# DLRM kernel: Z of four batches in one matmul, layer 0 of the preceding part between the halves

## Chip, cores and metric

The kernel runs on one core of a Trainium2 chip. The metric is the device time of one execution in microseconds. An engine here is TensorE (PE, its weight loads PEld), VectorE (DVE), ScalarE (ACT), GpSimd (POOL) or SyncE (SP).

## What is computed

A recommendation model for 2048 batches, all in float32. `_bn` normalizes over the batch.

```python
x = dense_inputs                                   # 2048 x 13
for W, b, g, be in bot:                            # 512, 256, 64
    x = _bn(jax.nn.relu(x @ W + b), g, be)
embs = tbl[idx]                                    # 26 tables of 12500 x 64, one row each per batch
T = jnp.concatenate([embs, x[:, None, :]], axis=1) # 27 x 64 per batch
Z = jnp.einsum('bnd,bmd->bnm', T, T)
R = jnp.concatenate([x, Z[:, iu, ju]], axis=1)     # upper triangle, 351 values
h = R
for W, b, g, be in top:                            # 512, 256, 1
    h = _bn(jax.nn.relu(h @ W + b), g, be)
return jax.nn.sigmoid(h)
```

## The kernel before

Each engine has its own instruction stream, written out by hand, in program order; semaphores tie them together. There is no planner.

**Start.** SyncE loads indices and weights (L288 to L300). VectorE turns indices into table rows and stages those of the first three parts (`stage_part`, L802), clears `Zs` (L814) and some constants. The bottom network runs over four chunks of 512 batches: layer 0 (L409), layer 1 with weights and activations split into two halves of the mantissa (`hi`, `lo`; L393, L399), layer 2 (L423). ScalarE does the relus (L610, L614, L582), VectorE the statistics (L827, L830, L720).

**Parts.** The 2048 batches are 16 parts of 128. GpSimd gathers the rows of a part with 26 indirect DMAs (L320; the last part L331) of 128 rows of 64 values each, in five loop passes of three parts (`LOOPS` = 5, `SLOTS` = 3 buffers `emb`) and the last part after it. A slot may be gathered into again once VectorE has run `stage_part` for it, which comes right behind the copies out of the transposes of the part that used it.

For each of the 15 parts in the loop:
- TensorE transposes 13 pairs of tables in four groups, each behind the landing of its gathers (L441), into two banks; VectorE copies each group to `TT` (L853); ScalarE adds the column of x (L636).
- TensorE multiplies: one matmul of 27 x 26 per batch (L455), 64 batches to a bank, the two halves h of the part from the lower and upper 64 rows of `TT`. The four column groups of the array take four batches side by side.
- Seven dummy matmuls keep TensorE working (`keep_clock`, L351), since its clock is granted by how it is used.
- VectorE and ScalarE take Z out of the banks into `Zs` (L254, L280), eight copies a half each.
- When all are taken, TensorE runs layer 0 of the top network on this part (L466 for x, L469 for the seven slices of `Zs`), four blocks of 128 outputs, each in a bank of its own. ScalarE writes two relus of each (L646, L648), VectorE statistics and the `lo` half (L864, L867).

**Last part.** It has a path of its own, in two halves of 64 batches (h = 0, 1) that are gathered one after the other: 13 gathers each, in groups of 8, 4 and 1 tables. Its transposes (h, g) are L479, its Z L493, its layer 0 L504 and L507 with batches as rows, transposed back by L516. The order on TensorE: transposes of half 0, Z 0, transposes (1,0), layer 0 of half 0, transposes (1,1) and (1,2), Z 1, layer 0 of half 1. Then comes the top network's layer 1 over all batches (L393, L399), layer 2 (L554), the normalization of the logits, the sigmoid (L699) and the store (L302).

**PSUM.** Eight banks: two for transposes, two for Z, four for layer 0, which also serve the dense layers as `out_bank`.

## Time and profile before

| | us |
|---|---|
| three timed runs | 589.98, 590.01, 588.6 (median 589.98) |
| profiled execution, span from first to last instruction | 987.2 |
| profiled execution, another time of its own | none on the page |
| TensorE busy in it | 448.2 (45%) |
| GpSimd busy | 401.1 (41%) |
| VectorE busy | 233.0 (24%) |
| ScalarE busy | 189.5 (19%) |

The profile is that of one execution, whose span is far longer than the timed runs. The timeline has for each run of like instructions its start, its length, the engine, the line, what it writes and reads, how many, and in brackets the idle time before it with what ended it.
### The profile page before, as it was taken

Reading aid. Unit: us, or ns where it says so; the run is one execution under the profiler, and the core shown is the slowest. Engines: PE = TensorE matmul, PEld = TensorE weight load, DVE = VectorE, ACT = ScalarE, POOL = GpSimd, SP = SyncE. Lnnn points to the kernel's source line nnn. Section 1 sums busy time; section 2 is a strip of 40 time slices with the busy share of each in tenths; the row PEclk is TensorE's granted clock in tenths of the full one; section 3 lists DMA queues with packets and bytes.
Section 4 is the critical chain, followed back from the end, with each engine's and each line's share of the span. In section 5 each row is a group of like instructions: output and inputs, shape, how many; then the busy total and the mean of one; then the engine's idle time right before and its main releaser. Section 6 shows DMA issues by size and latency. Waiting matters only on the chain.

```text
span 987.2 us, 13898 instructions
## 1 busy us (share of the span) xinstructions
PE 448.2 (45%) x5827; PEld 321.1 (33%) x5827; DVE 233.0 (24%) x640; ACT 189.5 (19%) x509; POOL 401.1 (41%) x426
## 2 busy tenths in 40 slices
PE   7751151624425161523517162351715244177787
PEld 3430020513214051412405051240514133165664
DVE  6600130402112040312204031220403022055542
ACT  5400020302011030302103030210303021044523
POOL 6777227072542707163361706336171634500000
PEclk9975575756657575755757575575757557577999
DMA  5122001020110202010110101011020101100000
GB/s 168 23 27 26 12 9 26 3 26 10 18 18 11 26 3 27 7 23 14 14 23 5 26 6 23 14 14 23 5 27 6 24 13 15 22 3 1 3 1 0
DMA packets 15895, 18.30 MB, mean 19 GB/s; under 512 B 7614, under 2 KB 8894, under 8 KB 15695
## 3 DMA queue, kind: packets, MB, share of 16 engines
q0 software_dynamic: 13312, 13.66, 10.6%
q1 hardware_dynamic: 2524, 3.72, 1.2%
q8 instruction: 53, 0.87, 0.4%
q14 instruction: 6, 0.05, 0.0%
HBM read 17.34 MB, written 0.01 MB: 18 GB/s over the span
## 4 chain that ended last, share of the span: by engine, by line
another core or an unknown queue 61%; PE 23%; ACT 10%; issue 3%; DVE 3%; DMA 0%; ACTq 0%; SPq 0%; DVEq 0%
PE l_bank L469 11%; ACT Zs L280 7%; PE l_bank L409 3%; PE l_bank L393 2%; PE l_bank L466 2%; PE l_bank L399 1%; PE l_bank L423 1%; ACT TT L636 1%; PE z_bank L455 1%; PE l_bank L507 1%; PE tr_bank L351 1%; DVE TT L853 1%; ACT hidden L582 0%; ACT hidden_hi L648 0%
## 5 line engine op out<-in xcount | busy, mean ns | idle before, releaser
L320 POOL DMA_INDIRECT emb<-table,stage x390 | 374.3, 960 | 424.1 <-DVE stage L802 309.2
L455 PE MATMUL z_bank<-TT 64*27 64x26 f32 x3840 | 127.5, 217 | 403.5 <-issue 388.4
L455 PEld LDWEIGHTS z_bank<-TT 64*27 64x27 f32 x3840 | 89.2, 132 | 442.9 <-issue 442.9
L254 DVE COPY Zs<-z_bank 27x112 f32<-27x112 f32 (+3 forms) x272 | 88.2, 324 | 498.7 <-remote 488.6
L280 ACT ACTIVATE Zs<-z_bank 27x112 f32<-27x112 f32 (+3 forms) x272 | 91.6, 337 | 552.8 <-remote 535.2
L469 PE MATMUL l_bank<-Zs,tw_sb 128*128 128x128 f32 x840 | 117.1, 298 | 0.0
L469 PEld LDWEIGHTS l_bank<-Zs,tw_sb 128*128 128x128 f32 x840 | 112.6, 215 | 0.0
L853 DVE COPY TT<-tr_bank 128x512 f32<-128x512 f32 (+1 forms) x60 | 51.1, 979 | 4.2 <-PE tr_bank L441 3.9
L351 PE MATMUL tr_bank<-idle_operand 128*128 128x512 bf16 x112 | 46.9, 590 | 0.0
L864 DVE BATCH_NORM_STATS2 stats_t<-h_block 128x128 f32 x60 | 17.7, 294 | 123.8 <-ACT hidden_hi L648 123.8
L441 PE MATMUL tr_bank<-ident,emb 128*128 128x128 f32 x195 | 30.8, 284 | 35.1 <-DVE TT L853 28.8
L646 ACT ACTIVATE h_block<-l_bank,par 128x128 f32<-128x128 f32 x60 | 22.0, 367 | 103.6 <-PE l_bank L469 103.6
L331 POOL DMA_INDIRECT emb<-table,stage x26 | 24.5, 944 | 34.0 <-DVE stage L802 26.3
L466 PE MATMUL l_bank<-x_all,twx_sb 128*128 x120 | 27.9, 318 | 21.7 <-ACT Zs L280 21.5
L340 POOL TENSOR_TENSOR hidden_lo<-h_block,hidden_hi 128x128 fp32r<-128x128 f32 x4 | 1.7, 454 | 88.2 <-ACT hidden_hi L681 88.2
L441 PEld LDWEIGHTS tr_bank<-ident,emb 128*128 128x128 f32 x195 | 21.9, 141 | 43.5 <-DVE TT L853 36.0
L393 PE MATMUL l_bank<-hidden_hi,w_hi 128*128 128x512 f32 x64 | 27.3, 426 | 17.4 <-issue 9.9
L466 PEld LDWEIGHTS l_bank<-x_all,twx_sb 128*128 128x128 f32 x120 | 21.0, 219 | 33.2 <-issue 33.2
L393 PE MATMUL l_bank<-hidden_lo,w_hi 128*128 128x512 f32 x64 | 26.6, 416 | 10.5 <-issue 10.5
L409 PE MATMUL l_bank<-hidden,bw_sb 13*128 13x512 f32 x32 | 27.7, 1061 | 5.4 <-DMA par<-params 5.4
L399 PE MATMUL l_bank<-hidden_hi,w_lo 128*128 128x512 f32 x64 | 19.8, 416 | 15.8 <-issue 15.8
L648 ACT ACTIVATE hidden_hi<-l_bank,par 128x128 f32 x60 | 21.6, 359 | 0.0
(120 smaller groups left out, 282.5 us busy)
## 6 DMA issues: line engine op xcount, KB each, us to landing
emb<-table,stage POOLq DMA_INDIRECT x416
tw_sb<-tw0x SPq DMA_DIRECT2D x1, 1792.0 KB
bw_sb<-bw SPq DMA_DIRECT2D x1, 512.0 KB
tw_sb<-tw SPq DMA_DIRECT2D x1, 512.0 KB
twx_sb<-twx SPq DMA_DIRECT2D x1, 256.0 KB
idx_raw<-idx SPq DMA_DIRECT2D x1, 169.0 KB, 3.0
bw_sb<-bw SPq DMA_DIRECT2D x2, 64.0 KB
hidden<-dense_t SPq DMA_DIRECT2D x1, 104.0 KB
```

The costliest lines, as they stand in the source:

```text
L254: last = copy(dst, src[:, :, ZC * q:ZC * q + w])
L280: return nc.scalar.activation(dst, src, ACT.Copy)
L320: pool.indirect_dma_start(out=emb[:, s, k, h, :], out_offset=None, in_=table, in_offset=bass.IndirectOffsetOnAxis(ap=stage[:, s, col:col + ...
L351: nc.tensor.matmul(bank[:, :], idle_operand[:, 0:P], idle_operand[:, :], start=True, stop=True)
L393: nc.tensor.matmul(bank, w1_scaled["hi"][:, k, o * P:(o + 1) * P], hidden0[part][:, k, ch * CHUNK:(ch + 1) * CHUNK], start=(n == 0 and par ...
L399: mm = nc.tensor.matmul(bank, w1_scaled["lo"][:, k, o * P:(o + 1) * P], hidden0["hi"][:, k, ch * CHUNK:(ch + 1) * CHUNK], start=False, sto ...
L409: nc.tensor.matmul(bank, bw0_sb[:, o * P:(o + 1) * P], dense_sb[:, ch * CHUNK:(ch + 1) * CHUNK], start=True, stop=True).then_inc(mm_done[" ...
L441: tr = nc.tensor.transpose(tr_bank[g % 2][:, c * P:(c + 1) * P], emb[:, s, k, :, :].rearrange("p h d -> p (h d)"), ident[:, :])
L455: mm = nc.tensor.matmul(bank[QUAD * j:QUAD * j + V, x * ZM:(x + 1) * ZM], one, one[:, 1:V], start=True, stop=True)
L466: nc.tensor.matmul(acc, twx_sb[:, cols], x_all[:, bass.ds(i * (2 * UNIT), 2 * UNIT)], start=True, stop=False)
L469: mm = nc.tensor.matmul(acc, tw0_sb[:, c, cols], Zs[:, c, :], start=False, stop=(c == ZC - 1))
L853: nc.vector.tensor_copy(TT[:, 0, :, n0:n0 + w].rearrange("p b n -> p n b"), tr_bank[g % 2][:, 0:w * UNIT].rearrange("p (n b) -> p n b", n= ...
```

## The change

The Z matmul takes four batches at once: stationary 128 columns (four batches of 32, `TT` padded from 27 to 32), moving 104 columns. The result is 128 x 104, and of it the four diagonal blocks of 27 x 26 are used. A part is cut in two sets of 64 batches, each of 16 such matmuls that alternate between the lower and upper 64 rows and are spread over four banks, so Z now has four banks. Layer 0 has two banks in the loop, taken in turn; blocks 2 and 3 wait for the relus of blocks 0 and 1. `Zs` gets three slots. TensorE's order becomes: transposes of part i, set 0 of i, layer 0 of part i-1, set 1 of i; the layer 0 of part 14 runs behind the loop. ScalarE and VectorE follow in the same order. The first three parts are written out ahead of a loop of four passes. The seven `keep_clock` matmuls of the loop are gone. The order of the batches within a part, of the dense inputs and of the output changes with it, so the sigmoid writes without a rearrangement. The last part's path keeps its operations.

```diff
-        TT = sb("TT", [P, 2, UNIT, V])
-        Zs = sb("Zs", [P, ZC, 2 * UNIT])
+        TT = sb("TT", [P, 2, UNIT, VP])
+        Zs = sb("Zs", [P, SLOTS, ZC, 2 * UNIT])
...
-        z_bank = [ps("z_bank%d" % k, [P, 512]) for k in range(2)]
-        l0_bank = [ps("l0_bank%d" % k, [P, 512]) for k in range(K0)]
+        z_set = ps("z_set", [P, ZB * 512])
+        z_bank = [z_set[:, k * 512:(k + 1) * 512] for k in range(ZB)]
+        l0_pair = [ps("l0_pair%d" % k, [P, 512]) for k in range(2)]
+        l0_bank = [l0_pair[0], l0_pair[1], z_bank[2], z_bank[3]]
...
+        def take_set(copy, s, t, quadrants):
+
+            for j in quadrants:
+                src = z_set[QUAD * j:QUAD * j + V, :].rearrange("p (k w) -> p k w", k=ZB)[
+                    :, :, 0:XB * NQ * ZM].rearrange("p k (u m) -> p k u m", m=NQ * ZM)
+                for q in range(NQ):
+                    w = quadrant_columns(q)
+                    dst = Zs[QUAD * q:QUAD * q + V, s, 0:w, t * UNIT:(t + 1) * UNIT].rearrange(
+                        "p c (k u j) -> p k u j c", k=ZB, j=NQ)[:, :, :, j, :]
+                    at = j * ZM + ZC * q
+                    last = copy(dst, src[:, :, :, at:at + w])
+            return last
...
+            def part_set(t):
+                for n in range(RX // SETS):
+                    k, g = divmod(n, XB)
+                    x = t * RX // SETS + n
+                    for h in range(2):
+                        four = TT[h * D:(h + 1) * D, 0, x * NQ:(x + 1) * NQ, :]
+                        mm = nc.tensor.matmul(z_bank[h * ZB // 2 + k][:, g * NQ * ZM:(g + 1) * NQ * ZM],
+                                              four.rearrange("p b n -> p (b n)"),
+                                              four[:, :, 1:V], start=True, stop=True)
+                mm.then_inc(z_done, 1)
+
+            def part_layer0(i, s):
+                for o in range(K0):
+                    cols = slice(o * P, (o + 1) * P)
+                    if o >= 2:
+                        pe.wait_ge(l0_relu, i * K0 + (o - 1))
+                    nc.tensor.matmul(l0_block_of(o), twx_sb[:, cols], x_all[:, bass.ds(i * (2 * UNIT), 2 * UNIT)],
+                                     start=True, stop=False)
+                    for c in range(ZC):
+                        mm = nc.tensor.matmul(l0_block_of(o), tw0_sb[:, c, cols], Zs[:, s, c, :],
+                                              start=False, stop=(c == ZC - 1))
+                    mm.then_inc(l0_done, 1)
+
+            def part(it, s, first=False):
+                i = it * SLOTS + s
+                part_transposes(it, i, s)
+                pe.wait_ge(tt_written, (i + 1) * GROUPS)
+                pe.wait_ge(tt_x_written, i + 1)
+                if not first:
+                    pe.wait_ge(z_taken_v, i * SETS)
+                    pe.wait_ge(z_taken_a, i * SETS)
+                pe.sem_inc(z_started, 1)
+                part_set(0)
+                if not first:
+                    if not (isinstance(i, int) and i == 1):
+                        pe.wait_ge(l0_relu, i * K0 - K0)
+                        pe.sem_inc(z_started, 1)
+                    part_layer0(i - 1, (s - 1) % SLOTS)
+                pe.wait_ge(z_taken_v, i * SETS + 1)
+                pe.wait_ge(z_taken_a, i * SETS + 1)
+                pe.sem_inc(z_started, 1)
+                part_set(1)
+
+            for s in range(SLOTS):
+                part(0, s, first=(s == 0))
+            with pe.Fori(1, LOOPS) as it:
                 for s in range(SLOTS):
...
-                    for h in range(2):
-                        bank = z_bank[h]
-                        for x in range(RX):
-                            for j in range(NQ):
-                                one = TT[h * D:(h + 1) * D, 0, x * NQ + j, :]
-                                mm = nc.tensor.matmul(bank[QUAD * j:QUAD * j + V, x * ZM:(x + 1) * ZM],
-                                                      one, one[:, 1:V], start=True, stop=True)
-                        mm.then_inc(z_done, 1)
-                    keep_clock(7, tr_bank[0])
...
+                    part(it, s)
+            pe.wait_ge(z_taken_v, LAST * SETS)
+            pe.wait_ge(z_taken_a, LAST * SETS)
+            pe.wait_ge(l0_relu, (LAST - 1) * K0)
+            part_layer0(LAST - 1, (LAST - 1) % SLOTS)
...
-            nc.scalar.activation(prob[:, :, :].rearrange("p b u -> p u b"),
-                                 logits[:, :].rearrange("p (u b) -> p u b", u=CU), ACT.Sigmoid,
+            nc.scalar.activation(prob[:, :], logits[:, :], ACT.Sigmoid,
...
-            nc.vector.memset(Zs[:, :, :], 0.0).then_inc(cleared, 1)
+            nc.vector.memset(Zs[:, :, :, :], 0.0).then_inc(cleared, 1)
+            nc.vector.memset(TT[:, :, :, V:VP], 0.0).then_inc(cleared, 1)
...
+            def part(i, s, first=False):
+                for g in range(GROUPS):
+                    n0, w = 2 * group_pairs(g)[0], 2 * len(group_pairs(g))
+                    dve.wait_ge(transposed, i * GROUPS + (g + 1))
+                    nc.vector.tensor_copy(
+                        TT[:, 0, :, n0:n0 + w].rearrange("p b n -> p n b"),
+                        tr_bank[g % 2][:, 0:w * UNIT].rearrange("p (n b) -> p n b", n=w),
+                    ).then_inc(tt_written, 1)
+
+                stage_part(s, bass.ds((i + SLOTS) * PW, PW))
+                dve.wait_ge(z_done, i * SETS + 1)
+                take_set(nc.vector.tensor_copy, s, 0, (0, 1)).then_inc(z_taken_v, 1)
+                if not first:
+                    part_stats(i - 1)
+                dve.wait_ge(z_done, i * SETS + 2)
+                take_set(nc.vector.tensor_copy, s, 1, (0, 1)).then_inc(z_taken_v, 1)
```

ScalarE's stream changes in the same way: x columns, takes of set 0, the relus of part i-1, takes of set 1, and the relus of part 14 behind the loop.

## Rows read from the trace of the kernel before

**Rows 1.** The page's first lines: span; busy us (share) and instructions.

```profile
span 987.2 us, 13898 instructions
...
PE 448.2 (45%) x5827; PEld 321.1 (33%) x5827; DVE 233.0 (24%) x640; ACT 189.5 (19%) x509; POOL 401.1 (41%) x426
```

**Rows 2.** The waits: engine, line, waited for: us in total, times, longest us.

```profile
PE z_bank L455 <- issue: 388.4, 368, 2.6
```

**Rows 3.** Timeline of PE, Z of part 1: start, us, engine, line, count, [idle before].

```profile
196.60 1.00 PE L455 MATMUL z_bank<-TT 64*27 64x26 f32 x67 [1.01 <-DVE TT L853]
...
220.58 0.20 PE L455 MATMUL z_bank<-TT 64*27 64x26 f32 x1 [2.60 <-issue]
```

**Rows 4.** Timeline of PE, part 14, no gather running; last line: a window, PEclk 0.50.

```profile
902.56 0.33 PE L441 MATMUL tr_bank<-ident,emb 128*128 128x128 f32 x1 [0.36 <-DVE TT L853]
903.90 1.71 PE L455 MATMUL z_bank<-TT 64*27 64x26 f32 x133 [1.01 <-DVE TT L853]
907.64 1.69 PE L455 MATMUL z_bank<-TT 64*27 64x26 f32 x123 [2.03 <-issue]
909.26 3.17 PE L351 MATMUL tr_bank<-idle_operand 128*128 128x512 bf16 x7
...
920.02 0.82 PE L479 MATMUL tr_bank<-ident,emb 128*128 128x128 f32 x6
...
904.00:912.00 8.00, 5.97 (x263) 3.89 (x262) 5.26 (x16) 5.37 (x16) 0.00 (x0) 0.50 0.02 4
```

**Rows 5.** Windows: us, busy of PE, PEld, DVE, ACT, POOL, PEclk, DMA share, GB/s.

```profile
57.00:108.00 51.00, 12.91 (x30) 6.75 (x28) 1.39 (x2) 1.37 (x2) 38.67 (x41) 0.56 0.20 26
...
950.00:973.00 23.00, 22.80 (x102) 18.55 (x103) 8.87 (x20) 5.36 (x10) 0.00 (x0) 1.00 0.00 1
```

**Rows 6.** Timeline of POOL: last of the first 78 gathers, first of the next.

```profile
107.00 0.94 POOL L320 DMA_INDIRECT emb<-table,stage  x1 [0.30 <-issue]
139.96 0.94 POOL L320 DMA_INDIRECT emb<-table,stage  x1 [32.01 <-DVE stage L802]
```

**Rows 7.** Timeline of PE: transposes (1,1), then (1,2), of the last part.

```profile
932.73 0.44 PE L479 MATMUL tr_bank<-ident,emb 128*128 128x128 f32 x2
933.00 0.27 PE L479 MATMUL z_bank<-ident,emb 128*64 128x128 f32 x1
```

**Rows 8.** Timeline, bottom layer 0: VectorE's L830 beside a gather.

```profile
17.98 0.67 DVE L830 TENSOR_TENSOR hidden_lo<-h_block,hidden_hi 128x512 fp32r<-128x512 f32 x1
18.07 1.39 POOL L320 DMA_INDIRECT emb<-table,stage  x1 [0.30 <-issue]
```

**Rows 9.** Timeline of PE, layer 0 blocks; windows: PE busy, PEclk the granted clock.

```profile
868.65 0.79 PE L466 MATMUL l_bank<-x_all,twx_sb 128*128 x2 [1.45 <-ACT Zs L280]
...
872.18 0.39 PE L466 MATMUL l_bank<-x_all,twx_sb 128*128 x2
...
873.96 0.39 PE L466 MATMUL l_bank<-x_all,twx_sb 128*128 x2
...
869.00:870.00 1.00, 1.00 (x6) 0.50 0.00 0
...
873.00:874.00 1.00, 1.00 (x12) 1.00 0.06 16
```

**Rows 10.** Timeline of ACT: eight takes of a half.

```profile
905.66 2.89 ACT L280 ACTIVATE Zs<-z_bank 27x112 f32<-27x112 f32 x8 [5.45 <-PE z_bank L455]
```

**Rows 11.** Timeline of DVE and POOL, start: clears, first statistics, a gather.

```profile
5.93 0.94 POOL L320 DMA_INDIRECT emb<-table,stage  x1 [0.31 <-issue]
6.01 0.81 DVE L814 MEMSET Zs<- 128x896 f32 x1 [0.25 <-DVE idx_clamped L797]
...
10.27 0.69 DVE L827 BATCH_NORM_STATS2 stats_b<-h_block 128x6 f32<-128x512 f32 x1 [2.81 <-ACT h_block L614]
```

**Rows 12.** Timeline of ACT, end: Square without, sigmoid with rearrangement.

```profile
980.80 0.72 ACT L694 ACTIVATE logit_sq<-logits,neg_mean 128x512 f32<-128x512 f32 x1 [0.73 <-DVE neg_mean L938]
...
983.68 1.30 ACT L699 ACTIVATE prob<-logits,norm_top 128x512 f32<-128x512 f32 x1
```

More of the change, by code:

```diff
@@ L68 @@
 ZM = NF
+VP = QUAD
+ZB = 4
+SETS = 2
+XB = 2 * RX // SETS // ZB
 CHUNK = 512
@@ new lines, in _, with part_relu @@
+            act.wait_ge(cleared, 2)
+            def part_relu(i):
+                for o in range(K0):
+                    act.wait_ge(l0_done, i * K0 + (o + 1))
+                    nc.scalar.activation(h0_part[:, o, :], l0_block_of(o), ACT.Relu,
+                                         bias=p_col("top", "b", 0)[:, o:o + 1]).then_inc(h0_f32, 1)
+                    nc.scalar.activation(hidden0["hi"][:, o, bass.ds(i * (2 * UNIT), 2 * UNIT)],
+                                         l0_block_of(o), ACT.Relu,
+                                         bias=p_col("top", "b", 0)[:, o:o + 1]).then_inc(l0_relu, 1)
@@ L653, in _ @@
+            for s in range(SLOTS):
+                part(s, s, first=(s == 0))
+            with act.Fori(1, LOOPS) as it:
+                for s in range(SLOTS):
+                    part(it * SLOTS + s, s)
+            part_relu(LAST - 1)
             for h in range(2):
@@ new lines, in part @@
+            def part(i, s, first=False):
+                for g in range(GROUPS):
+                    n0, w = 2 * group_pairs(g)[0], 2 * len(group_pairs(g))
[7 more added lines that the diff above has]
+                take_set(nc.vector.tensor_copy, s, 0, (0, 1)).then_inc(z_taken_v, 1)
+                if not first:
+                    part_stats(i - 1)
+                dve.wait_ge(z_done, i * SETS + 2)
+                take_set(nc.vector.tensor_copy, s, 1, (0, 1)).then_inc(z_taken_v, 1)
@@ L871, in last_stats @@
+            for s in range(SLOTS):
+                part(s, s, first=(s == 0))
+            with dve.Fori(1, LOOPS) as it:
+                for s in range(SLOTS):
+                    part(it * SLOTS + s, s)
+            part_stats(LAST - 1)
             def last_stats(o):
```

124 lines of the change are left out of this document (49 added, 75 removed).

## The prediction, before any run of the changed kernel

> **What bounds the kernel now.** I read the page first. Its span is 987.2 us, with TensorE busy 45% of it and GpSimd 41% [rows 1], and no other time stands on the page for this execution. The three timed runs have a median of 589.98 us, 397 us below that span, so the first question is what the profiled execution did that the timed ones can't have done.
>
> The waits answer it: TensorE stood idle before the Z matmuls of L455 for 388.4 us with nothing to wait for ("issue") [rows 2]. In the timeline the Z stage starts at full rate (67 records in 1.00 us), then crawls, at its worst with 2.60 us before a single record [rows 3]. The crawl lies where GpSimd issues gathers; the same stage of part 14, after the last gather, has one pause of 2.03 us [rows 4]. The bottom network's layer 1 crawls too: 30 matmul records in 51 us, while the same layer of the top network, with no gather about, does 102 in 23 us [rows 5]. A timed run 397 us shorter has no room for these stalls. I take them as something of the profiled execution alone.
>
> Without them, what is left? GpSimd. A gather takes 944 ns with 0.30 us before it, so one each 1.249 us. The 78 gathers of the first three parts end at 107.94 us. The next part waited in the trace for its slot until 139.96 us, 32.01 us long, because the bottom network was late [rows 6]. Unstalled, the crawling 30 records of the bottom network take 30/102 x 23 = 6.8 us instead of 51 [rows 5], so it ends at least 44 us earlier; the slot opens by 96 us, before 107.94, and GpSimd never waits. Then 338 more gathers run on to 108.2 + 338 x 1.249 = 530.4 us. From a part's last transpose to the next part's first one TensorE needs 17.4 us with no gather about (902.56 to 920.02 us [rows 4]), and a part's 26 gathers take 32.5 us: TensorE waits for landings, not the other way.
>
> After the last gather: its transpose stands at 933.00 us, the span ends at 987.2, so 54.2 us follow [rows 7]. 530.4 + 54.2 = 584.6 us. The 5.4 us up to the median hold the landing after the issue, what lies around the span, and gathers that meet a two-operand VectorE operation: in the bottom network they stretch to 1.40 us beside L830 [rows 8]. That this sum lands within 1% of the median is my best evidence that **the gather queue and the tail behind it bound the timed runs**.
>
> **The change, part by part.** All prices are from the profiled execution's rows; differences are added to the median, since the profiled span itself isn't comparable.
>
> *Z matmuls.* A part's 128 small matmuls (256 records, float32 makes two of each) become 32 of 104 columns (64 records). In the loop this is beside 32.5 us of gathers and worth nothing. The stage's own length: no row has this shape. A layer 0 record of 128 columns costs 3.53/16 = 0.22 us at the granted clock 0.50 (1.2 GHz) and 1.78/16 = 0.11 us at 1.00 (2.4 GHz) [rows 9], so a half (32 records of 104 columns) costs at most 5.7 or 2.9 us one after the other. But the old Z records overlap: 133 in 1.71 us at clock 0.50 is 13 ns each [rows 4], where streaming 26 columns at 1.2 GHz alone takes 22 ns. The new matmuls alternate between the two halves of the rows, so I take half: 2.8 us cold, 1.5 us warm, and keep the serial values for the range.
> The Trainium skill, page "TensorE: Matmul & The Clock Gate", section "Why this matters for your kernels", says that small-contraction matmuls in distinct row groups run concurrently. No row here shows row groups; by a rule of full concurrency the half is as I took it, and without it the sum would be 4.3 us higher.
>
> *keep_clock(7) removed:* 3.17 us of dummy matmuls a part [rows 4], which ran beside the copies. Worth nothing by itself; what it loses is that layer 0 starts at the low clock more often.
>
> *Layer 0 of the preceding part between the halves.* In the loop it stays under the gathers: per part about 25 us of TensorE chain (below) against 32.5. VectorE stages the slot's next rows as before, ahead of the takes, so GpSimd still never waits. *But at the end of the loop the order costs.* TensorE is in order, and the layer 0 of part 13 now stands behind the transposes of part 14, so behind its landing. Count t from the landing of part 14's last pair; the last part's final gather lands at 26 x 1.249 = 32.5, its group before at 31.2.
> Before: from that transpose (902.56) to the last part's first transposes (920.02) 17.4 us, on to its transposes (1,1) at 932.73 another 12.7 [rows 4, 7]. That is t = 30.1, before the landing at 31.2, so the gathers set the end: 32.5 + 54.2 = 86.7.
> After: 1.3 to the first half (902.56 to 903.90), 2.8 for it, then layer 0 of part 13: 3.5 for the first block cold and 3 x 1.8 [rows 9], making t = 13.0. ScalarE's eight takes (2.9 us [rows 10]) are done by 7.0, before the first block ends, so its relus don't hold the third block. Second half 1.5 warm, takes and handover 3.2: t = 17.7. Layer 0 of part 14, now wholly behind the takes: 2.8 for the first block, after 3 us of idling (between 1.8 warm and 3.5 cold, nearer the cold one) and 5.4: t = 25.9. The last part's first half then takes the unchanged 12.7: t = 38.6, past the last landing, and 54.5 more (932.73 to 987.2): 93.1. **The tail grows by 6.4 us.**
> Bounds: all at the high clock it is 4 us less; serial halves add 4.3; all of both layer 0s at the low clock would add 11 more, of which the range takes in the part up to 602.
>
> *Larger clears.* The memset of Zs takes 0.81 us and becomes three times that, the pads of TT (640 elements) some 0.6 us: 2.2 us more on VectorE, which is idle 2.81 us there before the first statistics [rows 11]. Hidden. If it held a gather up, 1 to 2 us would go straight to the end; beside the present memset the gather starting at 5.93 took 0.94 us as usual [rows 11], so I take 0. Waiting on `cleared` for 2 costs nothing by then.
>
> *Output order.* The sigmoid writes contiguously: 1.30 us now, against 0.72 us for a 128x512 Square without the rearrangement [rows 12]. It ends the chain: -0.6 us. Input layouts keep shapes and sizes: 0. The stride of TT going from 27 to 32 may move a copy's 0.98 us either way; in the loop it is hidden, in the tail few copies see it: 0, within 1 us.
>
> *Sum:* 589.98 + 6.4 - 0.6 = 595.8 us, about 1% slower.
>
> **Rivals.**
> *Slack hides it (no change).* If in the timed runs the part before last were landed earlier against the last gather than 32.5 us, or the half parts and layer 0 ran warm with shorter waits, the added layer 0 would fit. For this the new chain must shrink from 38.6 to under 32.5. For it: old chain (30.1) and landing (31.2) lie close together, and the new chain is a sum of six terms from other places. Against: a second layer 0 of over 7 us stands in a row, and the lowest bound still leaves 2.4 us. Or the old tail was already bound by TensorE, by some 5 us, which would explain the rest of 5.4 us between sum and median. Then 589.98 - 0.6 + 1 = 590.4. Chance 0.14.
> *TensorE bounds the loop in the timed runs too (faster).* If gathers are really quicker than the profile's 1.249 us and part of the "issue" stall is real, a part takes (590 - 96 - 67)/15 = 28.5 us now, with 96 as above and 67 the span from 920.02 to its end. The 32 matmuls cure the stall, a part falls to about 25 us (the chain above), and 15 x 3.5 = 53 us go: 537 us. This decides as soon as a gather takes under 28.5/26 = 1.10 us. Against it: all gathers outside the bottom network show 0.94 + 0.30 us to the hundredth. Chance 0.16.
> *The bigger matmuls save TensorE nothing:* three quarters of what they compute lies off the diagonal blocks and is unread. If they run one after the other at the low clock, a part's Z costs 11.5 us where the unstalled stage took about 5 [rows 4], and the time is some 600 us: the upper part of the forecast case, with its chance in it.
>
> **How the numbers follow.** The forecast case has 0.70, its own range 591.5 to 602. The range of 8 in 10 takes in the case without change: 588.5 to 602. The measurement can tell about 0.3% (1.8 us) from no change. Slower by more 0.70, within 0.14, faster 0.16.
>
> **What the profile of the changed kernel would show.** Right: gathers still spaced 1.249 us; TensorE's "issue" idle at Z far below 388 us, since a part leaves 141 matmul records instead of 340, and the span much nearer to the timed runs, which by itself says nothing of them. From the transpose of part 14's last pair to the last part's first transposes some 26 us where it was 17.4; the last part's transposes (1,1) without a wait for landing. Sigmoid near 0.7 us. Wrong: a timed result well under 588 us (gathers don't bound, or are quicker unprofiled); or the final gather landing after the first half of the last part was done, at a tail of 54 us behind it.

## The result, and the profile after

The changed kernel takes 595.73 us (median of four runs; its profiled execution 595.59), the kernel before 589.29 us (four runs). The ratio is 1.0100, 95% interval 1.0082 to 1.0118: slower by 1.0%, and by 6.4 us from median to median. One of the four runs was disturbed, at 811.9 us, and is not in the ratio; the median of the other three is 595.59. The unchanged kernel, profiled once more ("before, again"), has a span of 587.2 us where the first profile had 987.2, and its rows are used from here on. In every profile but that first one the time is 1.8 to 2.1 us above the span (595.59 for a span of 593.8, 589.28 for 587.2).

The page's first lines of the changed kernel, with the groups that answer to [rows 1, 2], and its chain of waits by engine. Columns as in [rows 1, 2]; in a group's row they are busy us, mean ns of one, and idle us ahead by what ended it.

```profile
span 593.8 us, 7908 instructions
...
PE 371.6 (63%) x2842; PEld 305.7 (51%) x2842; DVE 234.2 (39%) x641; ACT 190.8 (32%) x509; POOL 401.4 (68%) x426
...
POOL 62%; issue 21%; PE 10%; DVE 2%; ACT 2%; DMA 1%; POOLq 0%; DVEq 0%; ACTq 0%
...
L342 POOL DMA_INDIRECT emb<-table,stage x390 | 374.4, 960 | 121.8 <-issue 118.6
```

The waits of TensorE for landings in the changed kernel (us in total, times, longest):

```profile
PE tr_bank L461 <- DMA emb<-table,stage: 162.7, 33, 9.4
```

The same lines of the kernel before, profiled again:

```profile
span 587.2 us, 13898 instructions
...
PE 377.4 (64%) x5827; PEld 280.2 (48%) x5827; DVE 238.9 (41%) x640; ACT 190.5 (32%) x509; POOL 401.6 (68%) x426
...
PE tr_bank L441 <- DMA emb<-table,stage: 123.1, 27, 9.5
```

Two things are to be seen. TensorE's matmul records fell from 5827 to 2842, and its busy time by only 5.8 us, although 15 x 2.88 = 43 us of dummy matmuls are gone. The groups of the Z stage tell most of why, first before, again, then after (records, busy us, mean ns, idle ahead):

```profile
L455 PE MATMUL z_bank<-TT 64*27 64x26 f32 x3840 | 60.4, 220 | 32.9 <-issue 22.0 <-DVE TT L853 10.9
```

```profile
L472 PE MATMUL z<-TT 64*128 64x104 f32 x960 | 88.4, 355 | 14.0 <-DVE TT L917 11.0 <-ACT Zs L302 3.0
```

A quarter of the records, but 88.4 us of them in place of 60.4: the new Z stage is the longer one, even with the idle time counted in (102.4 against 93.3). The 28 us more of Z, and some 9 us more of layer 0 (L482 and L485 142.3 us, L466 and L469 133.1), take up most of the 43. TensorE now waits 162.7 us for landings instead of 123.1: what it was spared in the loop became waiting. The second is that the chain that ended last is gathers with the 0.30 us ahead of each (374.4 + 118.6 us, 83% of the span), then TensorE.

The two spans split at three places: the first one is the last transpose of part 14, the second one the last part's first transposes, the third one its transposes (1,1). Timeline of TensorE in the changed kernel, answering to [rows 4, 7] (start, us, engine, line, count, idle before):

```profile
499.35 0.47 PE L461 MATMUL tr_bank<-ident,emb 128*128 128x128 f32 x1 [1.37 <-DMA emb<-table,stage]
500.48 3.75 PE L472 MATMUL z<-TT 64*128 64x104 f32 x32 [0.65 <-DVE TT L917]
...
511.62 2.04 PE L472 MATMUL z<-TT 64*128 64x104 f32 x32
...
516.67 0.46 PE L482 MATMUL l_pair<-x_all,twx_sb 128*128 128x128 f32 x2 [3.02 <-DVE Zs L264]
...
525.52 0.82 PE L525 MATMUL tr_bank<-ident,emb 128*128 128x128 f32 x6
...
530.40 0.66 PE L525 MATMUL tr_bank<-ident,emb 128*128 128x128 f32 x4
...
540.10 0.44 PE L525 MATMUL tr_bank<-ident,emb 128*128 128x128 f32 x2
```

And the same of the kernel before, profiled again:

```profile
499.66 0.47 PE L441 MATMUL tr_bank<-ident,emb 128*128 128x128 f32 x1 [1.42 <-DMA emb<-table,stage]
500.72 2.08 PE L455 MATMUL z_bank<-TT 64*27 64x26 f32 x133 [0.59 <-DVE TT L853]
504.53 2.00 PE L455 MATMUL z_bank<-TT 64*27 64x26 f32 x123 [1.73 <-issue]
506.46 2.88 PE L351 MATMUL tr_bank<-idle_operand 128*128 128x512 bf16 x7
...
516.96 0.82 PE L479 MATMUL tr_bank<-ident,emb 128*128 128x128 f32 x6
526.12 1.11 PE L479 MATMUL tr_bank<-ident,emb 128*128 128x128 f32 x4 [3.90 <-DMA emb<-table,stage]
...
532.72 0.44 PE L479 MATMUL tr_bank<-ident,emb 128*128 128x128 f32 x2
```

| stretch, us | before, again | after | predicted for after |
|---|---|---|---|
| start to the last transpose of part 14 | 499.7 | 499.4 | no change |
| on to the last part's first transposes | 17.3 | 26.2 | 25.9 (17.4 before) |
| on to transposes (1,1) | 15.8 | 14.6 | 12.7 |
| on to the end of the span | 54.5 | 53.7 | 53.9 |

The last gather starts in both at the same time, first the kernel after, then before again (timeline of GpSimd):

```profile
529.24 0.95 POOL L353 DMA_INDIRECT emb<-table,stage  x1 [0.30 <-issue]
```

```profile
529.30 0.94 POOL L331 DMA_INDIRECT emb<-table,stage  x1 [0.31 <-issue]
```

So the loop neither gained nor lost. Before, TensorE waited 3.90 us for a landing at the transposes (1,0), at 526.12. They need the first eight gathers of the last half, the eighth of which is issued at 523.05:

```profile
523.05 0.94 POOL L331 DMA_INDIRECT emb<-table,stage  x1 [0.30 <-issue]
```

From 526.12 TensorE worked without a pause through layer 0 of half 0 to (1,1) at 532.72 and (1,2) at 533.00. So a landing set the tail, but not the last one: neither (1,1) nor (1,2) waited. After, (1,0) at 530.40 doesn't wait for a landing, and (1,1) stands 9.9 us behind the end of the last gather's issue (540.10 against 530.19), where it was 2.5 (532.72 against 530.24): the chain of TensorE and of the takes that it waits for sets the tail. The end has the sigmoid, answering to [rows 12], at 0.81 us against 1.30:

```profile
590.78 0.81 ACT L756 ACTIVATE prob<-logits,norm_top 128x512 f32<-128x512 f32 x1
```

### The profile page after: what moved, and what is told of

It is laid out like the page before. It is cut to its first block, busy times and chain, and to the rows that moved or that the text cites. A ratio compares the mean times of both kernels' runs of the same rounds, so it can differ in the third digit from the quotient of the medians.

```text
span 593.8 us, 7908 instructions
## 1 busy us (share of the span) xinstructions
PE 371.6 (63%) x2842; PEld 305.7 (51%) x2842; DVE 234.2 (39%) x641; ACT 190.8 (32%) x509; POOL 401.4 (68%) x426
## 4 chain that ended last, share of the span: by engine, by line
POOL 62%; issue 21%; PE 10%; DVE 2%; ACT 2%; DMA 1%; POOLq 0%; DVEq 0%; ACTq 0%
POOL emb L342 62%; PE l_pair L485 2%; PE l_pair L415 1%; PE z L415 1%; PE l_pair L553 1%; ACT Zs L302 1%; PE z L472 1%; PE z L421 1%; PE l_pair L421 1%; PE z L539 0%; DMA emb<-table,stage 0%; PE l_pair L482 0%; DVE Zs L264 0%; DVE moments_top L799 0%; DVE TT L291 0%
## 5 line engine op out<-in xcount | busy, mean ns | idle before, releaser
L342 POOL DMA_INDIRECT emb<-table,stage x390 | 374.4, 960 | 121.8 <-issue 118.6
L302 ACT ACTIVATE Zs<-z 27x112 f32<-27x112 f32 (+3 forms) x272 | 92.3, 339 | 259.6 <-PE z L472 253.2
L461 PE MATMUL tr_bank<-ident,emb 128*128 128x128 f32 x195 | 44.9, 363 | 175.2 <-DMA emb<-table,stage 162.7
L485 PE MATMUL l_pair<-Zs,tw_sb 128*128 128x128 f32 x840 | 113.4, 291 | 0.0
L264 DVE COPY Zs<-z 27x112 f32<-27x112 f32 x240 | 81.1, 338 | 76.2 <-PE z L472 73.4
L485 PEld LDWEIGHTS l_pair<-Zs,tw_sb 128*128 128x128 f32 x840 | 109.7, 210 | 0.0
L472 PE MATMUL z<-TT 64*128 64x104 f32 x960 | 88.4, 355 | 14.0 <-DVE TT L917 11.0
L472 PEld LDWEIGHTS z<-TT 64*128 64x128 f32 x960 | 82.4, 262 | 19.6 <-issue 17.9
L681 ACT ACTIVATE h_block<-l_pair,par 128x128 f32<-128x128 f32 x60 | 22.1, 368 | 55.1 <-PE l_pair L485 54.9
L482 PE MATMUL l_pair<-x_all,twx_sb 128*128 (+1 forms) x120 | 28.9, 328 | 3.0 <-DVE Zs L264 3.0
L482 PEld LDWEIGHTS l_pair<-x_all,twx_sb 128*128 128x128 f32 x120 | 21.1, 221 | 5.7 <-DVE Zs L264 3.2
L683 ACT ACTIVATE hidden_hi<-l_pair,par 128x128 f32 (+1 forms) x60 | 21.6, 360 | 0.0
L431 PE MATMUL l_pair<-hidden,bw_sb 13*128 13x512 f32 x16 | 14.6, 1066 | 5.6 <-DMA par<-params 5.6
```

The source lines that it names most:

```text
L264: last = copy(dst, src[:, :, :, at:at + w])
L302: return nc.scalar.activation(dst, src, ACT.Copy)
L342: pool.indirect_dma_start(out=emb[:, s, k, h, :], out_offset=None, in_=table, in_offset=bass.IndirectOffsetOnAxis(ap=stage[:, s, col:col + ...
L431: nc.tensor.matmul(bank, bw0_sb[:, o * P:(o + 1) * P], dense_sb[:, ch * CHUNK:(ch + 1) * CHUNK], start=True, stop=True).then_inc(mm_done[" ...
L461: tr = nc.tensor.transpose(tr_bank[g % 2][:, c * P:(c + 1) * P], emb[:, s, k, :, :].rearrange("p h d -> p (h d)"), ident[:, :])
L472: mm = nc.tensor.matmul(z_bank[h * ZB // 2 + k][:, g * NQ * ZM:(g + 1) * NQ * ZM], four.rearrange("p b n -> p (b n)"), four[:, :, 1:V], st ...
```

## The experiments

My theory: gathers carry the time up to the last landing; the change adds work of TensorE behind it, namely layer 0 of part 13. Rivals: the new Z matmuls are what costs (their length, or four banks that set 1 can't have before set 0 is taken); TensorE has a hand in the loop's time; the low clock in layer 0 of part 14 explains it.

### Is it the order or the new Z? (three kernels)

**Old order, new Z.** The changed kernel with layer 0 of part i-1 ahead of the transposes of part i. ScalarE's relus and VectorE's statistics move in the same way.

```diff
                 i = it * SLOTS + s
+                if not first:
+                    pe.wait_ge(z_taken_v, i * SETS)
+                    pe.wait_ge(z_taken_a, i * SETS)
...
+                    part_layer0(i - 1, (s - 1) % SLOTS)
                 part_transposes(it, i, s)
...
                 part_set(0)
-                if not first:
...
-                    part_layer0(i - 1, (s - 1) % SLOTS)
                 pe.wait_ge(z_taken_v, i * SETS + 1)
```

> The changed kernel, but layer 0 of part i-1 runs before the transposes of part i, on all three engines; the new Z matmuls, the two sets in the same four banks and all else stay. My theory (the tail grew through the order AND through two sets that wait for each other): counted from the transpose of part 14's last pair, 1.1 + set 0 3.7 + takes 3.1 + set 1 3.0 + takes 3.2 + layer 0 8.9 = about 23 us to the last part's first transposes, where the changed kernel has 26.2; so about 3 us less than the changed kernel, 592.5 us. Rival A (the order alone is to blame): all of it comes back, 588.7 us. Rival B (the bigger matmuls slow the whole loop): nothing comes back, 595.7 us.

Measured: 592.74 us against 588.84 of the kernel before on the same chip, ratio 1.0057 (1.0036 to 1.0078). Its timeline of TensorE:

```profile
499.31 0.47 PE L461 MATMUL tr_bank<-ident,emb 128*128 128x128 f32 x1 [1.36 <-DMA emb<-table,stage]
500.34 3.74 PE L472 MATMUL z<-TT 64*128 64x104 f32 x32 [0.56 <-DVE TT L918]
507.06 3.75 PE L472 MATMUL z<-TT 64*128 64x104 f32 x32 [2.98 <-ACT Zs L302]
...
523.41 0.82 PE L524 MATMUL tr_bank<-ident,emb 128*128 128x128 f32 x6
```

From the last transpose of part 14 to the last part's first ones it is 24.1 us, 6.8 above the 17.3 of before, although no second layer 0 stands there. Only 3.9 us of the 6.8 show in the time. The start is 0.3 us earlier, the next stretch is 1.5 us shorter, since its wait for a landing (3.90 us at 526.12 in before, again) is gone, and what follows is 1.1 shorter, half of it the sigmoid. Four banks for one set make set 1 wait for the takes of set 0, 2.98 us in the third line. The order before had one bank for each half and no such wait. The matmuls themselves add to it: the two sets take 7.5 us, the two halves of before 4.1.

**New order, old Z.** The changed kernel with the matmuls of 27 x 26, one bank for each half, still one half on each side of layer 0. The copies out of the banks are adapted to it.

```diff
             def part_set(t):
-                for n in range(RX // SETS):
-                    k, g = divmod(n, XB)
-                    x = t * RX // SETS + n
-                    for h in range(2):
-                        four = TT[h * D:(h + 1) * D, 0, x * NQ:(x + 1) * NQ, :]
-                        mm = nc.tensor.matmul(z_bank[h * ZB // 2 + k][:, g * NQ * ZM:(g + 1) * NQ * ZM],
-                                              four.rearrange("p b n -> p (b n)"),
-                                              four[:, :, 1:V], start=True, stop=True)
+                for x in range(RX):
+                    for j in range(NQ):
+                        one = TT[t * D:(t + 1) * D, 0, x * NQ + j, :]
+                        mm = nc.tensor.matmul(z_bank[t][QUAD * j:QUAD * j + V, x * ZM:(x + 1) * ZM],
+                                              one[:, 0:V], one[:, 1:V], start=True, stop=True)
```

> The changed kernel's order, banks, slots and layouts, but Z by the old matmuls of 27 x 26, one bank a half, taken half by half. My theory: the deferred layer 0 stays in the tail, so the chain is 1.1 + 2.5 + 9 + 2 + 3.2 + 8.9 = 26.7 us and the time that of the changed kernel, 595.7 us within 1. Rival (the bigger matmuls cost the time): back to about 589 us.

Measured: 594.26 us, ratio 1.0098 (1.0078 to 1.0117). That is a little below the window I had put down. Its timeline of TensorE:

```profile
498.81 0.47 PE L459 MATMUL tr_bank<-ident,emb 128*128 128x128 f32 x1 [1.42 <-DMA emb<-table,stage]
...
524.93 0.82 PE L520 MATMUL tr_bank<-ident,emb 128*128 128x128 f32 x6
```

26.1 us: with the new order the chain has its whole length with either form of Z.

**Both old**, in the frame of the changed kernel: `Zs` with three slots, `TT` with stride 32, the larger clears, three parts written out ahead of the loop, the new batch order and sigmoid, no dummy matmuls in the loop. The edit is the two above together, without the wait between the halves.

> Both taken back in the changed kernel's frame: layer 0 of part i-1 before the transposes of part i, old Z matmuls, the second half not waiting for the takes of the first. What stays of the change: padding, three slots of Zs, two banks for layer 0 in the loop, no keep_clock in the loop, batch order and a contiguous sigmoid. My theory: the tail chain is again about as long as the landing of the last gather leaves (30 to 32 us), so 589.3 - 0.5 for the sigmoid = 588.8 us, up to 1 us more for a colder layer 0. Rival (padding, slots, bank sharing or the missing dummy matmuls cost the time): above 592 us.

Measured: 588.43 us, ratio 1.0000 (0.9986 to 1.0014). Last transpose of part 14 to the next first ones: 17.8 us.

```profile
499.46 0.47 PE L459 MATMUL tr_bank<-ident,emb 128*128 128x128 f32 x1 [1.42 <-DMA emb<-table,stage]
...
517.25 0.82 PE L516 MATMUL tr_bank<-ident,emb 128*128 128x128 f32 x6
```

Everything else in the change is worth nothing together (within the interval of 0.14%; the sigmoid's 0.5 us is in it), so what is left is these two parts. The ratio is to the kernel before, run beside it; that of the changed kernel comes from another comparison (589.29 us for before) than those of the three others (588.84):

| | old Z | new Z |
|---|---|---|
| old order | 588.43 us, ratio 1.0000, chain 17.8 | 592.74 us, ratio 1.0057, chain 24.1 |
| new order | 594.26 us, ratio 1.0098, chain 26.1 | 595.73 us, ratio 1.0100, chain 26.2 |

Each alone costs 4 to 6 us, and together not the sum: in the new order, the ratios show no cost of the new Z. There, layer 0 of part 13 fills the time in which set 1 would wait for its banks. In the tail that is all that the reorder buys, and it is bought with a layer 0 there: 7.5 us for a wait of 3.

### Is it the clock in layer 0 of part 14?

Six dummy matmuls ahead of that layer 0, in the 3 us in which TensorE waits for the takes.

```diff
                     part(it, s)
+            keep_clock(6, tr_bank[0])
             pe.wait_ge(z_taken_v, LAST * SETS)
```

> The changed kernel with six dummy matmuls behind the loop, ahead of the wait for the last takes, where TensorE idles 3.0 us. My theory: layer 0 of part 14 takes 7.1 us instead of 8.9 and all of it shows in the end, since that layer 0 stands on the chain: 594.0 us, 1.7 less than the changed kernel. Rival (the last landing sets the end, the layer 0 is hidden): 595.7 us.

Measured: 593.90 us, ratio 1.0086 (1.0063 to 1.0110). From its timeline of TensorE:

```profile
514.79 1.47 PE L373 MATMUL tr_bank<-idle_operand 128*128 128x512 bf16 x6
517.87 0.46 PE L482 MATMUL l_pair<-x_all,twx_sb 128*128 128x128 f32 x2 [1.61 <-DVE Zs L264]
...
525.09 0.82 PE L526 MATMUL tr_bank<-ident,emb 128*128 128x128 f32 x6
```

That layer 0 now takes 7.2 us (517.87 to 525.09) instead of 8.85, as expected. How much of it reaches the time is less sure: the median is 1.8 us below that of the changed kernel, but the ratios, 1.0086 and 1.0100, have intervals that overlap. At most 1.8 us of the 6.4 are the clock here; the rest is not.

### Do the two row halves of TensorE work side by side?

The changed kernel with the 16 matmuls of a set in another order: eight of the lower 64 rows, then eight of the upper. Same work, same banks.

```diff
-                for n in range(RX // SETS):
-                    k, g = divmod(n, XB)
-                    x = t * RX // SETS + n
-                    for h in range(2):
+                for h in range(2):
+                    for n in range(RX // SETS):
+                        k, g = divmod(n, XB)
+                        x = t * RX // SETS + n
```

> The changed kernel with the 16 matmuls of a set ordered by half: eight on the lower 64 rows, then eight on the upper, instead of alternating. If neighbouring matmuls overlap because they sit in different rows of the array, a cold set grows from 3.7 to about 5.7 us and a warm one from 2.0 to 2.9, and the tail by 2 to 4 us: 597.5 to 599.5 us. If the overlap doesn't come from that, set and time stay: 595.7 us.

Measured: 603.48 us against 589.99, ratio 1.0237 (1.0212 to 1.0263), which is 7.7 us over the changed kernel and more than I expected. From its timeline of TensorE:

```profile
500.52 0.47 PE L461 MATMUL tr_bank<-ident,emb 128*128 128x128 f32 x1 [1.42 <-DMA emb<-table,stage]
501.64 6.40 PE L472 MATMUL z<-TT 64*128 64x104 f32 x32 [0.65 <-DVE TT L917]
...
516.88 3.46 PE L472 MATMUL z<-TT 64*128 64x104 f32 x32
...
532.96 0.82 PE L525 MATMUL tr_bank<-ident,emb 128*128 128x128 f32 x6
```

A set costs 6.40 us cold and 3.46 warm; alternating, 3.75 and 2.04. Taking turns makes the same matmuls 1.7 times as fast, at either clock (PEclk 0.50 for the cold sets, 1.00 for the warm ones). That the rows alone do it isn't shown: each row half writes its own two banks, so matmuls that take turns between row halves take turns between PSUM banks as well. My serial bound (5.7 and 2.9 us, from layer 0 records of 128 columns) was itself 12 to 20% low. Of the 6.2 us by which the chain is longer (32.4 against 26.2), the two sets are 4.1; layer 0 between them took 8.9 us (507.97 to 516.88) instead of 7.5, that behind them 9.6 instead of 8.85, and the last gather came 1 us late.

### Does TensorE have a hand in the loop?

The kernel before with 21 dummy matmuls where it has 7.

```diff
-                    keep_clock(7, tr_bank[0])
+                    keep_clock(21, tr_bank[0])
```

> The kernel before with 21 instead of 7 dummy matmuls a part, 14 x 0.22 to 0.44 us = 3 to 6 us more on TensorE behind Z in each part, of which some 1 lies under the takes. My theory: hidden under the gathers 14 times, seen once, in part 14, less the slack of 1 to 2 us before the last landing: 590 to 594 us. Rival (TensorE bounds the loop): 15 x 3 to 6 us more, 630 to 680 us.

Measured: 592.44 us against 589.99, ratio 1.0039 (1.0017 to 1.0061), in five runs between 588.28 and 593.67. The profiled one is that of 588.28. Timelines of TensorE, then GpSimd:

```profile
504.97 6.29 PE L351 MATMUL tr_bank<-idle_operand 128*128 128x512 bf16 x21
```

```profile
528.87 0.95 POOL L331 DMA_INDIRECT emb<-table,stage  x1 [0.30 <-issue]
```

3.4 us more for each of 15 parts (6.29 against 2.88) is 51 us of dummy matmuls. TensorE's busy time grew by 39.9 us (417.3 against 377.4), since transposes and layer 0 took less (L441 36.9 for 41.9 us, L469 103.6 for 106.0), and its waits for landings at L441 fell from 123.1 to 89.8 us. The last gather is where it was: in the loop TensorE has time to spare. Where the median lost 2.4 us can't be read from a profile whose own run lost nothing, and stays open.

### Is a gather's issue the price of the loop?

The other side: the kernel before with one more gather for each of the 15 loop parts, into a buffer of its own, ahead of the part's last transpose.

```diff
                             ).then_inc(landed[s][k // GROUP], 16)
+                    pool.indirect_dma_start(
+                        out=extra_rows[:, s, :], out_offset=None, in_=table,
+                        in_offset=bass.IndirectOffsetOnAxis(ap=stage[:, s, 25:26], axis=0),
+                    ).then_inc(landed[s][GROUPS - 1], 16)
```

> The kernel before with one more gather in each of the 15 parts of the loop, into an unused tile; the last group's transpose waits for it too. My theory (gathers bound the timed runs of the kernel before): 15 x 1.249 = 18.7 us more, 608 us. Rival (TensorE bounds its loop): about 589 to 591 us.

Measured: 607.60 us against 588.77, ratio 1.0317 (1.0293 to 1.0341): 18.8 us, where 15 x 1.249 = 18.7. The last gather starts 18.9 us later:

```profile
548.16 0.95 POOL L336 DMA_INDIRECT emb<-table,stage  x1 [0.30 <-issue]
```

**The kernel before, again**, unchanged, for a profile that is worth reading:

> The kernel before, unchanged, profiled once more. My theory (the idle time marked issue in the profile shown belongs to that one execution, not to the kernel): the span is now near 587 us, the issue stall at the Z matmuls is gone, GpSimd issues without a wait, and the tail from the transpose of part 14's last pair to the last part's first transposes is about 17 us. Rival (records of 256 Z matmuls a part always stall a profile): a span near 987 us again.

Measured: 588.42 us, ratio 0.9997 (0.9984 to 1.0009). Its rows stand above. A part leaves 340 records, as before, and the crawl of [rows 2, 3] is gone: 22.0 us of "issue" at L455, where it was 388.4. Why the first profiled execution crawled isn't known.

### Why are some gathers 1.40 us long?

In the bottom network gathers last 1.40 us beside L830 [rows 8]. There the gather queue itself could be shortened. L830 subtracts two operands that both lie in SBUF. The kernel before, with ScalarE's relu of layer 0 written to a PSUM bank that is free then, so that one operand comes from there:

```diff
-                nc.scalar.activation(h0_block[:, n % 2, :], bank, ACT.Relu,
+                nc.scalar.activation(z_bank[n % 2][:, 0:CHUNK], bank, ACT.Relu,
...
-                nc.vector.bn_stats(stats["bot", 0][:, o, ch, :], h0_block[:, n % 2, :])
+                nc.vector.bn_stats(stats["bot", 0][:, o, ch, :], z_bank[n % 2][:, 0:CHUNK])
...
-                nc.vector.tensor_tensor(hidden0["lo"][:, o, cols], h0_block[:, n % 2, :],
+                nc.vector.tensor_tensor(hidden0["lo"][:, o, cols], z_bank[n % 2][:, 0:CHUNK],
```

> The kernel before, but in the bottom network's layer 0 ScalarE writes the float32 relu into the two idle Z banks instead of the block in SBUF, so the subtraction on VectorE that makes lo has only one operand in SBUF. My theory (a gather can't start while a VectorE operation with two SBUF operands runs, and gathers bound the kernel): the gathers of 1.40 us become 0.94, 17 x 0.46 = 7 to 8 us less, if the tail follows: 581.5 to 583 us. Rival A (the stretch has another cause, the weight loads for one): gathers still at 1.40, 589 us. Rival B (gathers don't bound): gathers at 0.94 and 589 us all the same.

Measured: 584.20 us against 589.99, ratio 0.9904 (0.9884 to 0.9925). The lines that answer to [rows 8], in its timelines of GpSimd and VectorE, and its last gather:

```profile
18.32 0.94 POOL L320 DMA_INDIRECT emb<-table,stage  x1 [0.30 <-issue]
523.28 0.94 POOL L331 DMA_INDIRECT emb<-table,stage  x1 [0.30 <-issue]
...
17.91 0.67 DVE L830 TENSOR_TENSOR hidden_lo<-z_bank,hidden_hi 128x512 fp32r<-128x512 f32 x1
```

The subtraction itself is as long as before, 0.67 us. The gather beside it falls from 1.40 us (1.39 in [rows 8]) to 0.94, the last gather starts 6.0 us sooner (523.28 against 529.30), and the time follows by 5.8. Over the whole loop the gathers are busy 368.8 us (mean 946 ns) instead of 374.8. I had expected 7 to 8 us, from 17 stretched gathers; in before, again, 13 last 1.34 us or more, which gives the 6.0.

The edit also moves ScalarE's write and the read of the statistics out of SBUF, so by itself it doesn't say which of the three mattered. The gathers of before, again, do. Of 15 that start while L830 runs, 13 are stretched. Of 11 that start while L867 runs, which subtracts two SBUF operands too but is only 0.27 us long, four are, to 1.00 to 1.04 us. The 12 that start beside the statistics of L864, with one operand in SBUF, and the 30 that start beside ScalarE's relus L646 and L648, take 0.94 to 0.95.

### Put together

**Old Z, old order, relu in PSUM**, in the frame of the changed kernel:

> old_z_old_order and before_relu_in_psum together. My theory: both effects stand side by side, the gathers end 5.8 us earlier and the sigmoid saves 0.5: 582.9 us, ratio to before 0.989 or less. Rival (the tail's TensorE chain, no longer than the landing by a hair, takes over): 584 to 585 us.

Measured: 582.72 us, ratio 0.9888 (0.9869 to 0.9907).

**The same with the clock kept up:** the seven dummies of the loop back, and 14 instead of 5 ahead of the last half's layer 0.

```diff
                 part_set(1)
+                keep_clock(7, tr_bank[0])
...
             last_z(1)
-            keep_clock(5, tr_bank[1])
+            keep_clock(14, tr_bank[1])
```

> psum_and_old_order with the seven dummy matmuls a part back, and 14 instead of 5 behind the last Z, where TensorE idles 1 to 3 us ahead of the last layer 0, whose 28 records took 3.2 us in two profiles and 1.7 in another. My theory: part 14's layer 0 warm (7.5 instead of 8.6 us) and the last one warm (1.5 less, on the chain for sure): 581.5 us. Rival (the dummy matmuls delay what they warm): 583 us or more.

Measured: 581.61 us against 588.77, ratio 0.9875 (0.9852 to 0.9898). The slices of the last half's layer 0, first in the kernel with both old, then in this one:

```profile
539.09 3.27 PE L544 MATMUL l_pair<-tw_sb,Zs 128*64 128x128 f32 x28
```

```profile
534.20 1.73 PE L545 MATMUL l_pair<-tw_sb,Zs 128*64 128x128 f32 x28
```

28 records in 1.73 us instead of 3.27 (3.23 in the version without the additions). That the dummies did it isn't settled: in the profile with the relu in PSUM alone, with five dummies, they took 1.73 us as well. The two additions together bring 1.1 us of median over the version without them, which the intervals don't tell apart. This version beats both kernels: 1.2% under the one before, some 2.2% under the changed one (0.9875 / 1.0100 = 0.978).

## Why the prediction was right

The forecast was 595.8 us; 595.73 came. The steps, one by one:

**Gathers bound the loop: right, and shown.** One more gather a part costs its 1.249 us (18.8 of 18.7 us); 51 us more of dummy matmuls leave the last gather in place; the removal of half of TensorE's records gave nothing. The last gather ends at 530.24 us in before, again; my sum had 530.4. The 5.4 us from the sum of 584.6 to the median, which I spread over three causes, now have numbers: 2.8 us from the end of the last gather's issue to the transposes (1,2) (530.24 to 533.00), 2.1 around the span (589.28 to 587.2), and 0.7 because the three runs I had lay that much above the median of the four taken in the end, less 0.2 of the issue.

**How the old tail hung on the gathers: wrong in the path.** I let the end wait for the last landing, with TensorE ready for (1,1) before it. But (1,2) starts right behind (1,1), with no idle time. What held TensorE was the landing of the eighth gather of the half (3.90 us of waiting, to 526.12), with 6.6 us of its own work behind it up to (1,1). So the 2.8 us above are not a landing time; the transposes (1,0) start 2.1 us behind the end of the issue that they wait for (526.12 against 523.99). By the same 2.1 us the last gather would have landed at about 532.3 (an estimate, from 530.24), within 1 us of (1,2) at 533.00. That the two paths lie so close is luck, and is why the old tail still came out at 86.7 for 87.6.

**The profile's stalls were of that execution alone: right; why they would go was wrong.** I wrote that the "issue" idle would fall "since a part leaves 141 matmul records instead of 340". The unchanged kernel, profiled again, leaves all its records and has a span of 587.2 us. The number of records was not the cause; what was, stays open. The conclusion that carried the sum, that a run 397 us shorter had no room for them, needed no cause.

**The tail's chain: right, term by term within 1.4 us.** TensorE from the last transpose of part 14, as forecast and as found:

| term, us | forecast | measured |
|---|---|---|
| first set, cold | 2.8 | 3.7 |
| its end to the end of layer 0 of part 13 | 8.9 | 7.5 |
| start of the second set, from the transpose | 13.0 | 12.3 |
| second set, warm | 1.5 | 2.0 |
| takes and handover | 3.2 | 3.0 |
| layer 0 of part 14 | 8.2 | 8.9 |
| all, to the next transposes | 25.9 | 26.2 |

The errors are of both signs and cancel: the sets are a third longer than I took them (next point), layer 0 of part 13 ran warmer than I priced it. That they cancel is luck. The window of the first set shows the low clock, that ahead of the last layer 0 a mixed one (columns as in [rows 5]):

```profile
500.00:504.00 4.00, 3.52 (x32) 3.52 (x32) 0.26 (x2) 0.00 (x0) 2.85 (x4) 0.50 0.18 25
...
516.60:519.00 2.40, 2.33 (x16) 2.36 (x17) 0.00 (x0) 0.00 (x0) 1.89 (x2) 0.79 0.24 33
```

PEclk 0.50 is 1.2 GHz; the set stands behind waits for landings. 0.79 is a mix of both levels, in a window that begins where the engine had idled for 3.02 us.

**Row halves side by side: right in direction, mis-sized.** I took half of the serial cost. The gain is 1.7 and not 2, on a serial cost 12 to 20% above my bound, and the banks change along with the row halves. The Trainium skill, page "TensorE: Matmul & The Clock Gate", section "Why this matters for your kernels", has small-contraction matmuls in distinct row groups run concurrently. The traces agree in that taking turns saves time (6.40 against 3.75 us), though not to the half.

**The first half of the last part: mis-sized by 1.9 us.** I carried 12.7 us over unchanged; it was 14.6. From the changed kernel's timeline of TensorE:

```profile
528.65 1.82 PE L539 MATMUL z<-TT 64*27 64x26 f32 x128 [0.69 <-DVE TT L289]
...
534.38 0.44 PE L550 MATMUL l_pair<-twx_sb,x_all 128*64 128x128 f32 x4 [2.89 <-ACT Zs L302]
534.62 2.81 PE L553 MATMUL l_pair<-tw_sb,Zs 128*64 128x128 f32 x28
```

In the profile that I had, the same 128 Z records took 1.29 us and the 28 of layer 0 1.73. From its first record to the transposes (1,1), layer 0 took 5.7 us (534.38 to 540.10) where it had been 4.1, Z 0.5 more, and what stands before Z 0.3 less. The longer layer 0 goes with the clock: a granted 0.63 over 534.4 to 537.1, where it had been 1.00. The prediction allowed for a low clock in the layer 0s of parts 13 and 14, not here. The longer Z does not: its records ran at a granted 1.00 both times. They take 1.69 to 1.82 us in the profiles in which GpSimd is still issuing gathers at that point, among them before, again, with 1.80, and 1.29 us where it no longer is, in the profile that I had and in the one without taking turns (gathers end at 531.21, Z starts at 536.08). No run shows why.

**How the sum closes.** From the last transpose of part 14 to the end, I had 86.7 us before, and 93.1 less 0.6 after. It was 87.6 (17.3 + 15.8 + 54.5) and 94.5 (26.2 + 14.6 + 53.7). So both tails were longer than I had them, by 0.9 and 2.0 us; the difference is 6.9 us where I had 5.8. That the forecast lies within 0.1 us is luck: I started from a median of before that was 0.7 us too high, the stretch up to part 14 is 0.3 us shorter after, and the time around the span 0.3 us less.

**Clears and sigmoid: right.** VectorE still idles before the first statistics, 1.26 us instead of 2.81 [rows 11]; the two clears take 2.1 us more (2.30 and 0.59 against 0.81), and the last gather starts at the same time. From the changed kernel's timeline of VectorE:

```profile
5.55 2.30 DVE L870 MEMSET Zs<- 128x2688 f32 x1 [0.63 <-DVE idx_clamped L853]
...
10.44 0.69 DVE L884 BATCH_NORM_STATS2 stats_b<-h_block 128x6 f32<-128x512 f32 x1 [1.26 <-ACT h_block L660]
```

The sigmoid gave 0.49 us where I took 0.6.

**What I did not see.** In the prediction the new Z alone was worth nothing, and all the cost was in the order. The old order with the new Z loses 3.9 us too. I priced the matmuls, at a third too little, but not that a set of 64 batches over four banks takes away the second buffer: in the order before, TensorE worked on the second half while the first was being taken. In the full change that wait is covered by the very layer 0 that I did price, so the forecast of the full change didn't need it.

**The rivals.** *Slack hides it:* no; TensorE needs 40.8 us from that transpose to (1,1) (26.2 + 14.6), and the last landing was there by 33.3 at the latest, since (1,2) ran then in before, again (499.66 to 533.00). *TensorE bounds the loop:* no, by the two experiments on the loop. *The bigger matmuls save TensorE nothing:* true of its busy time (88.4 us against 60.4), though not at the price of 600 us that I gave it; the form without taking turns costs 603.5, and taking turns avoids that.

## What to carry to other kernels

When a queue bounds the loop, work of other engines is free there as long as it fits, and costs its length behind the last items of the queue, less what slack the tail had: software-pipelining a stage by one part puts one more stage into the tail. Letting the last part run in the old order should avoid that; no run here tried it. A larger matmul form can cost time if it takes the second buffer away (592.74 us against 588.43 in the old order); count the banks before the instructions. When a tail seems to wait for the last transfer, look at which landing the engine idled for. And when a profile's span is far above the timed runs, take it again before explaining any of its waits.

## What the runs showed of the hardware that I had not expected

- A gather's issue on GpSimd takes 1.40 us instead of 0.94 if it starts while VectorE subtracts two operands in SBUF, and 0.94 again when one of them lies in PSUM, with the subtraction unchanged at 0.67 us. The Trainium skill, page "SBUF — State Buffer", section "Who interferes with whom", has such an operation of two SBUF inputs contend with GpSimd's reads, and reports a probe in which it did not stall DMAs. For these indirect DMAs the runs show that it does.
- The copies of VectorE from PSUM into `TT` got faster when the row stride went from 27 to 32 values, at the same size: the median fell from 1153 to 1011 ns. The kernel with old Z and old order, which keeps only the stride and the frame, has 1011 as well. The lines by source (count: shortest, median, longest ns), of the kernel before, again, and of the changed one:

```profile
L853 DVE COPY TT<-tr_bank x60: 405/1153/1197, 80.9 to 500.2; 128x512 f32<-128x512 f32 x45, 128x128 f32<-128x128 f32 x15
```

```profile
L917 DVE COPY TT<-tr_bank x60: 361/1011/1062, 81.9 to 499.9; 128x512 f32<-128x512 f32 x45, 128x128 f32<-128x128 f32 x15
```

- Z in a quarter of the matmuls keeps TensorE busy for longer, 88.4 us against 60.4: the small ones, of which four lie in the four column groups, already went by in 2.0 to 2.1 us for 64 batches at the low clock, with some 1.7 us of pause between the halves, and the large ones take 3.75 us at that clock and 2.04 at the high one.
- 128 of the small Z records take 1.7 to 1.8 us while GpSimd issues gathers and 1.3 us when it doesn't, at the same granted clock of 1.00.
